# Heads on partition mod 32: the bonus joins the sums on VectorE ahead of the transposes, one bonus product, one replica of v, queues reordered

## What is computed

```
# block 0, per element (C = 128 channels, T = 512)
A  = softmax((Wn inorm(x) + bn)^T (Wm inorm(ctx) + bm))
x  = Wo (Wl ctx + bl) A^T + bo + x
# block 1 (L = 128 steps, E = 512, H = 32 heads of 16), state rows from ctx
xa = ln(x);  sx = previous xa - xa
xk, xw, xv, xr, xg = xa + sx * (maa_stack + low-rank mix)
w  = exp(-exp(time_decay + tanh(xw td_w1) td_w2));  r, k, v = xr Wr^T, xk Wk^T, xv Wv^T;  g = silu(xg Wg^T)
for each step t and head:  a = k_t v_t^T;  out_t = r_t (u * a + s);  s = a + w_t * s
x1 = x + (groupnorm(out per head) * g) Wo^T
out = x1 + sigmoid(.. Wfr^T) * (square(relu(.. Wfk^T)) Wfv^T)
```

## Time and profile before

| | |
|---|---|
| median of 3 runs | 1774.38 us |
| profiled execution | 1773.87 us |
| its span, first to last instruction | 1772.1 us |
| PE, weight loads, DVE | 98%, 70%, 92% busy |
| ACT, POOL | 67%, 53% busy |
| mean granted TensorE clock | 0.991 of full |

### The profile page before, as it was taken

How to read it: one execution, slowest core, us unless ns; L and a number is a source line. 1 busy time by engine, 2 the same in 40 slices (tenths; PEclk the granted TensorE clock), 3 DMA queues, 4 the chain that set the end, 5 groups by cost and what they waited for, 6 DMA issues and landing times.

```text
span 1772.1 us, 33090 instructions
## 1 busy us (share of the span) xinstructions
PE 1728.8 (98%) x11570; PEld 1234.0 (70%) x11570; DVE 1636.2 (92%) x2224; ACT 1180.4 (67%) x2952; POOL 935.7 (53%) x752
## 2 busy tenths in 40 slices
PE   8899999999999999999999999999999999999878
PEld 6667667677767677767767766767776777776646
DVE  3699999999999999999999999999999999999993
ACT  4665677676667676667767667767666777666543
POOL 1344556555655654655655555665465565555540
PEclk9999999999999999999999999999999999999989
DMA  6343343343333344334344433334333334433420
GB/s 257 82 102 105 93 105 94 99 120 97 100 103 99 91 114 106 104 91 104 93 104 115 102 92 107 94 95 120 100 99 101 98 94 110 101 93 94 104 84 13
DMA packets 81732, 180.82 MB, mean 102 GB/s; under 512 B 18304, under 2 KB 35072, under 8 KB 80544
## 3 DMA queue, kind: packets, MB, share of 16 engines
q1 hardware_dynamic: 59920, 161.93, 35.0%
q10 hardware_dynamic: 21648, 16.78, 3.1%
HBM read 161.91 MB, written 16.78 MB: 101 GB/s over the span
## 4 chain that ended last, share of the span: by engine, by line
PE 84%; DVE 10%; issue 3%; ACT 1%; POOL 1%; DMA 0%; SPq 0%; DVEq 0%; POOLq 0%; ACTq 0%
PE bank L2014 29%; PE bank L2021 17%; PE bank L2138 6%; PE bank L2059 5%; PE bank L2046 5%; PE bank L2026 5%; PE bank L2095 4%; PE bank L2033 3%; DVE S L873 2%; PE bank L2074 2%; DVE A L855 2%; DVE A L885 2%; PE bank L2116 1%; PE bank L2149 1%; PE bank L2039 1%
## 5 line engine op out<-in xcount | busy, mean ns | idle before, releaser
L855 DVE TENSOR_TENSOR A<-vrep,kt 128x1008 f32<-128x1008 f32 x256 | 311.3, 1225 | 2.5
L560 POOL COPY S<-s 128x16 f32<-128x16 f32 x128 | 81.7, 639 | 419.0 <-DVE A L885 418.8
L873 DVE TENSOR_TENSOR_SCAN S<-wrep,S 128x512 f32<-128x512 f32 x256 | 299.7, 1212 | 1.2 <-issue 0.2
L885 DVE TENSOR_TENSOR A<-S,rt 128x2048 f32<-128x2048 f32 x128 | 292.0, 2282 | 0.1
L534 POOL TENSOR_TENSOR xf<-xf,xa 128x512 f32<-128x512 f32 x160 | 223.1, 1396 | 39.2 <-DVE xf L811 39.1
L1496 ACT ACTIVATE bank<-bank,par 128x128 f32<-128x128 f32 x640 | 173.4, 366 | 39.9 <-PE bank L2095 39.3
L503 POOL TENSOR_TENSOR hrs<-hrs,mhalf 128x32 f32<-128x32 f32 x31 | 171.0, 5517 | 2.6
L552 POOL TENSOR_TENSOR rk<-rT,kT 128x256 f32<-128x256 f32 x32 | 105.9, 3311 | 103.7 <-DVE oc L910 103.7
L501 POOL TENSOR_SCALAR rstd<-mv 128x1 f32<-128x1 f32 (+1 forms) x96 | 73.8, 769 | 156.9 <-DVE mv L748 61.4
L863 DVE TENSOR_TENSOR S<-A 128x1008 f32<-128x1008 f32 x128 | 155.5, 1215 | 0.2
L811 DVE TENSOR_TENSOR xf<-bank,sx 128x512 f32<-128x512 f32 x160 | 108.2, 677 | 44.7 <-PE bank L2014 22.7
(11 more groups left out here) (165 smaller groups left out, 4093.1 us busy)
## 6 DMA issues: line engine op xcount, KB each, us to landing
vrep<-v_dram SPq DMA_DIRECT2D x256, 512.0 KB
xc<-x_c SPq DMA_DIRECT2D x32, 256.0 KB, 6.5
xs<-x_s SPq DMA_DIRECT2D x32, 256.0 KB, 7.2
v_dram<-vT ACTq DMA_DIRECT2D x32, 256.0 KB, 3.1
out<-rr ACTq DMA_DIRECT2D x31, 256.0 KB, 2.7
st<-state SPq DMA_DIRECT2D x64, 2.0 KB, 6.4
Wv<-big_w SPq DMA_DIRECT2D x1, 1024.0 KB, 7.3
Wk<-big_w SPq DMA_DIRECT2D x1, 1024.0 KB, 9.0
```

The source lines that it names most:

```text
L855: ve_.tensor_tensor(A[:, u % 2, half * WJ:(half + 1) * WJ, 0:P - 2], vrep[:, half, :, 0:P - 2], k, ALU.mult).then_inc(dve_outer.sem, 1)
L873: last = ve_.tensor_tensor_scan(s, w, s, 0.0, ALU.mult, ALU.add)
L885: ve_.tensor_tensor(out4, s, r, ALU.mult).then_inc(dve_read.sem, 1)
```

## The change

Three things. (1) Weights, u, decay and state rows are permuted on the host (`by_value`) so that head h lies on the partitions h, 32 + h, 64 + h, 96 + h of every chunk; a chunk holds four of each head's 16 rows. One replica of v (2 halves) then serves all four chunks, one mask all four sums, and the bonus product's rows of the four chunks can be added up before PE. (2) The bonus is added to the sums by DVE (`tail_o4`), and only the total is transposed. r is copied once more by ACT, scaled by u. (3) All queues have a new order; the step begins elsewhere and spans six elements (b0 to b5).

```diff
-    "O:1 Rp:2 V:0 G:2 Tx:1 Mn:0 Mm:0 W1:1 S0:0 Wt:1 S1:0 S2:0 Mv:1 Mw:1 S3:0 Mk:1 Mr:1 Mg:1 Vp:1 "
-    "D1:1 Kp:1 T0:0 T1:0 T2:0 D2:1 E2:1 T3:0").split())]
+    "T1:1 T2:1 T3:1 O:1 D2:2 E2:2 Kp:2 Rp:2 G:2 Tx:1 Mn:0 Mm:0 W1:1 V:0 Wt:1 S0:0 S1:0 Mv:1 Mw:1 "
+    "S2:0 S3:0 Mk:1 Mr:1 Mg:1 Vp:1 D1:1 T0:0").split())]
-    "Tx2:4 FK:4 C:3 C2:3 FR:4 FV:4 Tg:3 Wo:3").split())]
+    "Tx2:4 FK:4 FR:4 FV:4 Tg:3 Wo:3 C:2").split())]
...
# SP
-            def load_vrep(n, p, v):
+            def load_vrep(n, p, half):
-                v1 = held(sp, regs[1], dve_outer.count(f"a{(v - 2) % V}", n if v >= 2 else n - 1))
+                v1 = held(sp, regs[1], dve_outer.count(f"a{V - 2 + half}", n - 1))
-                             src[u][:, half * WJ * P:(half + 1) * WJ * P].unsqueeze(1).broadcast_to([HC, HS, WJ * P]))\
+                             src[:, half * WJ * P:(half + 1) * WJ * P].unsqueeze(0).broadcast_to([C, H, WJ * P])).then_inc(vrep_loaded[half], 16)
             def step(on):
+                b0, b1, b2, b3, b4, b5 = on
+                load_st0(b3[0], b3[2])
+                load_vrep(b3[0], b3[2], 1)
+                load_x(b0[0] + 1, 1 - b0[2])
+                load_vrep(b2[0], b2[2], 0)
+                load_st1(b1[0], b1[2])
+                load_s0(b1[0], b1[2])
...
# POOL
-                po.tensor_tensor(rku[:, :, :], rT[:, :, :], kT[:, :, :], ALU.mult).then_inc(pool_wkv.sem, 1)
+                po.tensor_tensor(rkc[:, :, 0:P], rkc[:, :, 0:P], kT[:, :, :], ALU.mult).then_inc(pool_wkv.sem, 1)
+            def wkv_rks(n, m, p):
+                eng.wait_ge(pool_wkv.sem, pool_wkv.count("rk", n))
+                eng.wait_ge(pool_rk2.sem, pool_rk2.count("rk2", n))
+                po.tensor_tensor(rkc[:, 0:2, :], rkc[:, 0:2, :], rkc[:, 2:4, :], ALU.add).then_inc(pool_rks.sem, 1)
+                eng.wait_ge(pool_rks.sem, pool_rks.count("half", n))
+                po.tensor_tensor(rkc[:, 0, :], rkc[:, 0, :], rkc[:, 1, :], ALU.add).then_inc(pool_rks.sem, 1)
...
# DVE
-                ve_.tensor_tensor(bonus[:, :], vT[:, p, :, :].rearrange("p c t -> p (c t)"), bank_of("C")[:, :],
+                ve_.tensor_tensor(by_chunk(oc[:, :]), vT[:, p, :, :],
+                                  bank_of("C")[:, 0:P].unsqueeze(1).broadcast_to([P, C, P]), ALU.mult).then_inc(dve_bonus.sem, 1)
+            def tail_o4(n, m, p):
+                eng.wait_ge(pe_wkv.sem, pe_wkv.count(f"r{U - 1}", n))
+                eng.wait_ge(pe_tail.sem, pe_tail.count("Tx2", n - 1))
+                eng.wait_ge(dve_bonus.sem, dve_bonus.count("ob", n))
+                ve_.tensor_tensor(o4, by_chunk(bank[SUM_BANK][:, :]), by_chunk(oc[:, :]), ALU.add).then_inc(dve_sum.sem, 1)
...
# ACT
-                eng.dma_start(v_dram[p].rearrange("(c e) t -> e c t", c=C), vT[:, p, :, :]).then_inc(v_stored, 16)
+                eng.dma_start(v_dram[p].rearrange("(h g c) t -> g h (c t)", h=H, c=C), vT[:, p, :, :].rearrange("e c t -> e (c t)")).then_inc(v_stored, 16)
# in mid_r, ahead of the copy to rT
+                eng.wait_ge(pe_bonus.sem, pe_bonus.count("C", n - 1))
+                for c in range(C):
+                    sc.activation(rkc[:, c, 0:P], bank_of("Rp")[:, c * P:(c + 1) * P], ACT.Copy, scale=col("u", c))
-                sc.activation(o4, by_chunk(bank[SUM_BANK][:, :]), ACT.Copy).then_inc(act_tail.sem, 1)
...
# PE
-                ones = slide[:, HC * (3 - u):HC * (7 - u)]
+                ones = head_rep[:, 0:H]
-                    last = pe.matmul(bank[SUM_BANK][32 * g:32 * g + 32, :], ones, A[:, u % 2, g:UJ:4, :],
+                    last = pe.matmul(bank[SUM_BANK][32 * g:32 * g + 32, :], ones, A[:, u % 2, C * g:C * g + C, :],
-                for c in range(C):
-                    last = pe.matmul(bank_of("C")[:, c * P:(c + 1) * P], head_u[:, c, :], rku[:, c, :],
-                                     start=True, stop=True)
-                pe.matmul(bank_of("C2")[:, 0:C * T2], head_rep[:, :], rk2[:, :, :].rearrange("p c m -> p (c m)"),
+                pe.matmul(bank_of("C")[:, 0:P + T2], head_rep[:, :], rkc[:, 0, :], start=True, stop=True).then_inc(pe_bonus.sem, 1)
-                for k in range(4):
-                    pe.matmul(o[:, k], o4[:, k, :], ident[:, :], start=(k == 0), stop=False, is_transpose=True)
-                eng.wait_ge(dve_tail.sem, dve_tail.count("ob", n))
-                for c in range(C):
-                    last = pe.matmul(bank[O_BANK][:, c * P:(c + 1) * P], bonus[:, c * P:(c + 1) * P], ident[:, :],
-                                     start=False, stop=(c == C - 1), is_transpose=True)
+                for k in range(C):
+                    last = pe.transpose(o[:, k], o4[:, k, :], ident[:, :])
```

More of the change, by code:

```diff
@@ L35 @@
 CONSTS = 14
-LAGS = 5
+LAGS = 6
 FIRST, LAST = 5, NB - 1
@@ L1129, in opening @@
[L1129 to L1138 removed]
+                wkv_pair(*at(1), 3)
+                att_aggr(*at(4))
+                tail_mix(*at(0), 0)
+                wkv_scan(*at(1), 3)
+                mid_kw(*at(2))
@@ new lines, in opening @@
+                att_rstd(*at(4))
+                mid_rw(*at(2))
+                wkv_read(*at(1), 3)
+                tail_ob(*at(1))
+                wkv_outer(*at(2), 0)
+                mid_gate(*at(2))
+                tail_o4(*at(1))
+                mid_s0(*at(3))
+                mid_shift(*at(3))
+                wkv_outer(*at(2), 1)
+                mid_xx(*at(3))
+                wkv_pair(*at(2), 0)
+                tail_mix(*at(0), 1)
+                tail_var(*at(1))
+                wkv_outer(*at(2), 2)
@@ L1177, in step @@
-            def step(on):
-                b0, b1, b2, b3, b4 = on
-                wkv_pair(*b3, 3)
+            def step(on):
+                b0, b1, b2, b3, b4, b5 = on
+                tail_gn(*b4)
+                fin_y(*b5)
+                att_max(*b1, 3)
+                wkv_scan(*b3, 1)
+                tail_gate(*b4)
+                wkv_read(*b3, 1)
+                att_rinv(*b1, 2)
+                wkv_outer(*b3, 4)
+                att_rinv(*b1, 3)
+                wkv_outer(*b3, 5)
+                mid_mix(*b2, 2)
+                mid_mix(*b2, 3)
+                wkv_pair(*b3, 2)
+                mid_mix(*b2, 4)
+                tail_x1(*b4)
+                tail_o(*b3)
+                tail_o2(*b3)
+                tail_st(*b4)
@@ L1194, in step @@
+                tail_rstd(*b4)
+                wkv_read(*b3, 2)
+                wkv_pair(*b3, 3)
+                att_xag(*b1)
+                wkv_scan(*b3, 3)
+                wkv_read(*b3, 3)
+                mid_s0c(*b2)
                 att_rstd1(*b1)
                 att_stats(*b0)
+                tail_mix(*b4, 0)
                 att_aggr(*b0)
+                mid_kw(*b2)
+                tail_mix(*b4, 1)
+                wkv_outer(*b2, 0)
+                tail_o4(*b3)
+                mid_gate(*b2)
@@ L1197, in step @@
+                mid_s0(*b1)
+                att_rstd(*b0)
+                wkv_outer(*b2, 1)
+                mid_shift(*b1)
+                mid_xx(*b1)
                 wkv_pair(*b2, 0)
-                tail_mix(*b4, 1)
+                tail_var(*b3)
+                mid_rw(*b2)
                 wkv_scan(*b2, 0)
-                tail_o(*b3)
-                mid_gate(*b2)
-                att_rstd(*b0)
                 wkv_outer(*b2, 2)
-                mid_shift(*b1)
-                tail_o2(*b3)
@@ L1428, in _ @@
             eng.wait_ge(pool_const, 9)
-            def head_scale():
-                for c in range(C):
-                    sc.activation(head_u[:, c, :], head_rep[:, :], ACT.Copy, scale=col("u", c)).then_inc(act_setup, 1)
             def att_norm(n, m, p, i):
@@ L1951, in closing @@
                 tail_xc2(*at(29), 0)
                 tail_xc2(*at(29), 1)
+                mid_r(*at(31))
                 fin_store(*at(28))
-                mid_r(*at(31))
+                tail_sq(*at(30))
+                fin_kr(*at(29))
+                mid_th(*at(31))
+                fin_kk(*at(29))
+                fin_rr(*at(29))
+                decay(*at(31), 1)
                 decay(*at(31), 2)
                 decay(*at(31), 3)
-                fin_kr(*at(29))
-                tail_o4(*at(30))
```

1244 lines of the change are left out of this document (566 added, 678 removed).

## The result

The changed kernel takes 1790.55 us (median of 4, 1786.80 to 1793.89), the kernel before 1774.28 us beside it (median of 4): ratio 1.0093, 95% interval 1.0072 to 1.0114. It is slower by 0.9%; 1745 us were forecast, and the range ended at 1764. The profiled execution took 1793.89 us, its span 1792.1, against 1773.87 and 1772.1 before. It is the slowest of the four: the medians are 16.3 us apart, the profiled spans 20.0.

A forecast was written before the change was run, and what follows sets the result against it. PE was taken to bound the kernel, at 52.52 us a lap. Thirty laps at 51.6 us save 27.6 and the drain 1.3: 1772.1 - 28.9 + 1.8 = 1745 us; 8-in-10 range 1728 to 1764.

The forecast's parts named there:

- The start, "even": Opening: four ACT scalings of 0.3 us go, the centring of Wv on DVE becomes four instructions; no net change.
- PE's lap, 51.03: PE's time per element: bonus work of 1.96 us replaced by one 0.47 us matmul, 52.52 to 51.03 us.
- DVE, 51.1 to 51.4, and the engines changing places: DVE's lap: the 0.60 us add gives 51.10 us, 51.4 with its own gaps, above PE's, so DVE bounds.
- POOL, 0.2 us of holding: In each lap, POOL's two new additions (0.96 and 0.48 us) hold DVE instructions with two SBUF inputs by 0.2 us.
- Transfers and order: Fewer replica loads gain nothing and land in time; the new queue order's rings stay near 51.3 us a lap.
- rival 4: DVE's outer 1 waits for v's replica from a 9.9 us landing on; at 11.5, lap 54.1, time 1822 us; chance 0.06.
- The sum: Laps' saving: 30 PE-full laps, each going from 52.52 to 51.6 us, give 27.6 us.
- The drain, −1.3: End of the program: bonus products and four transposes go, a 0.60 us DVE add comes; 1.3 us less.
- Rival 1 to 3: Lap 51.1, 1729 us, chance 0.18; POOL holds DVE, lap 52.2, 1763, 0.20; PE not the bound, 1774, 0.06.

The follow-up runs named there:

- e1: The changed kernel with the mean over s0 (mid_s0 of element 0) moved later in DVE's opening, just ahead of mid_shift (late s0): 1768.52 us, ratio 0.9976.
- e2: The kernel before with one wait added: DVE waits for element 0's load of s0 after the first aggregation; 1792.42 us, ratio 1.0112.
- e8: e1 with the load of x for element 3 asked for ahead of v's replica for element 1 in the opening: 1767.53 us, ratio 0.9964.
- e9: e8 with the centring of Wv moved behind element 0's last row sum in DVE's opening: 1762.11 us, ratio 0.9951.
- e12: e9 with element 30's last part put earlier in the closing, on POOL and likewise on the other engines: 1760.39 us, ratio 0.9935.
- e6: e1 with the sums copied out by ACT as before and no add on DVE, bonus left out of the output: 1770.04 us, ratio 0.9985.
- e7: e1 with POOL's two additions moved ahead of its second mix add: 1781.74 us, ratio 1.0048.
- e5: e1 without POOL's two additions, so the bonus of three of the four chunks is missing: 1767.35 us, ratio 0.9964.

## Why the prediction was wrong

**The start, "even": failed, and decided the sign.** The step counted instructions ("four ACT scalings go, the centring becomes four instructions") and not which queue each stands in behind what. It cost 21.7 us at xin(0); moving the instruction gives 17.9 of them back (e1), and the wait alone puts 19.4 on the kernel before (e2). The diff showed mid_s0(0) ahead of att_rstd(0), the profile its load behind 8 MB of weights. With that wait gone, element 5 was still 14.0 us late (e1); the load of x for element 3 ahead of a replica took 8.4 of them (e8), the centring 3.0 (e9), and 2.6 are left in e9 and 0.2 in e12, which has e9's opening. So a single trace fixes these shares to 2 or 3 us only. What is left isn't settled: the first outer products wait 4.9 us for the replica in e8 (at 78.65 and 83.54).

**PE's lap, 51.03: mis-sized by 0.28.** The product is 0.33 us (0.47 was taken, bounds 0.22 to 0.63); the 0.42 us of group changes were not in the sum. The sum matmuls stayed at 3.83 us for 32, as said.

**DVE, 51.1 to 51.4, and the engines changing places: size right, conclusion wrong.** DVE is busy 51.41 us, tail_o4 takes 0.68 and 0.60 in the queue. But e6 takes 0.6 us off DVE and the lap stays, so PE bounds it still, with DVE level (e7). PE's idle time, forecast at 0.5 us a lap, is 0.06.

**POOL, 0.2 us of holding: mechanism right, size and place wrong.** The additions are 0.99 and 1.39 us (0.96 and 0.48 were said). They hold a scan by 0.68, which e5 shows to be all but free; the mix that was held by 0.40 before takes 0.68 us now. What counts is a product that was there before, ez, which meets nmr in 13 of the 24 laps: 0.43 us each. The second product fell from 3.88 to 0.84 us in its new place.

**Transfers and order.** The replica is in time in all but two laps, where DVE waits 0.5 us: rival 4 fell, but by less than was said. In the lap of 929 us the load had not landed 9.8 us after its issue, where 4 to 5 us were taken (2 of transfer, 2 to 3 of way) and from 9.9 on rival 4 was to decide. The lap is 51.74 us on average without the long one, against 51.6 forecast; partly luck, as PE's floor came out 0.28 higher and DVE's holds cost less than assumed. The 24 laps gave 18.7 us at that mean and 14.41 with the long lap, where 0.92 each make 22.1. The sum counted 30 laps; from element 5 to 29 there are 24.

**The drain, −1.3: failed, +5.95.** 2.5 us are lost before xin(31), 3.4 from it to x1(31); 3.2 of the 3.4 lie behind the last hvar, 13.96 us to x1(31) against 10.79 before. The step took from the drain what the bonus gives and left out what the new closing order costs. Element 30's rstd (6.7 us on POOL) started 0.5 us after its hvar before and 5.8 us after it in e9 (a late-s0 kernel with after's closing), behind a copy that waits for a read of element 31. Moving it (e12) brings hvar to x1 down to 10.2 us, but the reads end 3.1 us later, and under 1 us is left of it. So where the 3.4 us come from is shown only in place, not in cause; the 2.5 us of the two last laps no run tries.

**The rivals.** Rival 1 to 3 all took the two ends for given, and rival 4 put its one slow mechanism into the lap. The one that came true, a wait in the opening, was on no list. How often the long lap of 56 us comes isn't known: none of the other eleven traces of kernels with the new order has one (their longest lap between elements 5 and 29 is 53.0 us).

## What to carry to other kernels

A wait in the opening is paid once and nearly in full (22.8 us of waiting cost 20 in e2): for each instruction that a change moves there, ask which load it waits for, where that load stands on its queue, and what is behind the instruction. When an order is rewritten, put the start, the laps and the drain down as three sums and walk each engine's queue in all three. Where two engines are both near full, the chain of waits over a whole lap tells which one bounds it, and taking work from the other (e5, e6) is the test.

## What was not expected of the hardware

A group of matmuls on PE takes longer behind some groups than behind others: 32 projection matmuls 3.77 us behind the small matmuls of the mixes or the decay and 3.57 behind all others, four transposes 0.59 us behind sum matmuls and 0.44 behind all others. A new order thus changed the floor of the bound engine by 0.42 us a lap. This is read from the chain of waits of before and e6; no run changes PE's order alone.

Whether POOL holds DVE turns on hundredths of a microsecond: the same ez costs nmr 0.43 us where it begins 0.04 us ahead, and nothing otherwise, so laps come mostly in two lengths, 51.29 and 51.72. The Trainium skill ("SBUF — State Buffer", Who interferes with whom) has the exclusion as a rule, and the trace agrees with it: nmr reads two inputs in SBUF and took 0.58 us in place of 0.15. Which hold is paid for is another matter: 0.68 us on a scan cost next to nothing, 0.43 on nmr are in the lap whole.

Loads of 2 KB and 32 KB took 11.4 us (st, behind a half replica and two x loads) and 20 us (s0, behind 8 MB of weights) from issue to landing. The 2 KB of st took 20.3 us behind the same weights (issued at 10.33) and 1.8 with nothing ahead (at 59.94): the queue ahead of them, not their size, sets it.
